# Attention rounds with whole-row maxima, strips of 256 queries, and the value products of two key tiles together at the end of a round

## The reference, cut to what matters

```python
B, S, D = X.shape                      # 1, 1024, 256
H, Dh = 16, 16
Xn = (X - mu) * rsqrt(var + 1e-5) * ln_w + ln_b
Q, K, V = split(Xn @ W_in, 3)          # each (16 heads, 1024, 16)
Q, K = _rope(Q), _rope(K)              # first half of the channels is rotated
scores = einsum('bhqd,bhkd->bhqk', Q, K) / sqrt(16)
probs = softmax(scores, axis=-1)
ctx = einsum('bhqk,bhkd->bhqd', probs, V)
out = ctx @ W_out + X
...                                    # the later stages are not changed
```

## Time and profile before

| what | value |
|---|---|
| time, median of 3 runs | 1087.62 us (1085.27 to 1093.72) |
| profiled execution, first to last instruction (its span) | 1084.3 us |
| median time less that span | 3.3 us |
| first query-side score (L519), first key-side score (L533) | 28.0 us, 48.3 us |
| first and last value product (L547) | 53.5 us, 231.7 us |
| busy over the span: PE, DVE, ACT, POOL | 95%, 73%, 62%, 47% |

### The profile page before, as it was taken

How to read it: one execution, slowest core, us unless ns; L and a number is a source line. 1 busy time by engine, 2 the same in 40 slices (tenths; PEclk the granted TensorE clock), 3 DMA queues, 4 the chain that set the end, 5 groups by cost and what they waited for, 6 DMA issues and landing times. The chain is left out here.

```text
span 1084.3 us, 18619 instructions
## 1 busy us (share of the span) xinstructions
PE 1028.1 (95%) x6437; PEld 812.5 (75%) x6437; DVE 787.5 (73%) x1789; ACT 673.7 (62%) x1235; POOL 507.1 (47%) x457
## 2 busy tenths in 40 slices
PE   7999999989999997799999999999889999999997
PEld 5433333347888986699988998899789778888997
DVE  5789999836766856898999999998567465333843
ACT  4478888756544447788778878787456344333454
POOL 3252331114058561767686777777506000536544
PEclk9989999999999998899999999999899999999999
DMA  4533434205224300351113121221011123655100
GB/s 91 91 64 56 76 54 68 70 13 164 78 70 136 49 2 23 113 181 64 55 64 113 59 65 54 93 73 39 2 36 28 44 57 88 159 159 163 67 20 21
DMA packets 80633, 79.28 MB, mean 73 GB/s; under 512 B 29320, under 2 KB 67676, under 8 KB 80540
## 3 DMA queue, kind: packets, MB, share of 16 engines
q1 hardware_dynamic: 80228, 77.66, 27.0%
q10 hardware_dynamic: 312, 0.43, 0.3%
HBM read 65.51 MB, written 1.28 MB: 62 GB/s over the span
## 5 line engine op out<-in xcount | busy, mean ns | idle before, releaser
L682 ACT ACTIVATE attn_probs<-attn_rows_k 128x512 f32<-128x512 f32 x256 | 134.4, 605 | 37.2 <-PE attn_rows_k L533 37.0
L770 DVE TENSOR_REDUCE attn_row_max<-s_sum 128x1 f32<-128x512 f32 x171 | 111.8, 682 | 15.9 <-PE s_sum L519 13.3
L533 PE MATMUL attn_rows_k<-attn_q_stack,attn_k_stack 50*128 50x512 f32 x256 | 96.9, 465 | 5.7 <-ACT attn_probs L682 5.6
L2865 DVE TENSOR_TENSOR late_mids<-late_mids,late_bank 128x512 f32<-128x512 f32 (+1 forms) x50 | 34.4, 687 | 78.8 <-PE late_bank L67 75.8
L65 PE MATMUL late_bank<-net_x_part_low,late_w_T 128*128 128x512 f32 (+1 forms) x192 | 77.9, 406 | 0.0
L66 PE MATMUL late_bank<-net_x_part_low,late_w_T 128*128 128x512 f32 (+1 forms) x192 | 76.1, 396 | 0.0
L67 PE MATMUL late_bank<-net_x_part_low,late_w_T 128*128 128x512 f32 (+1 forms) x192 | 76.0, 396 | 0.0
L519 PE MATMUL s_sum<-attn_k_stack,attn_q_stack 48*128 48x512 f32 x171 | 72.8, 470 | 1.9 <-DMA attn_q_stack<-s_part 1.4
L1530 POOL TENSOR_TENSOR gold_mids<-gold_mids,s_later 128x512 f32<-128x512 f32 x32 | 51.9, 1659 | 46.2 <-DMA s_later<-gold_weights 46.2
L2770 ACT ACTIVATE late_mids<-late_bank 128x512 f32<-128x512 f32 (+1 forms) x50 | 29.9, 597 | 69.6 <-PE late_bank L67 69.5
L2966 POOL TENSOR_TENSOR late_mids<-late_mids,late_raw_w_T_last 128x512 f32<-128x512 f32 x22 | 29.8, 1378 | 89.7 <-DMA late_raw_w_T_last<-top_weights 89.7
(11 more groups left out here) (459 smaller groups left out, 3491.9 us busy)
## 6 DMA issues: line engine op xcount, KB each, us to landing
lin_mix<-decay_sums SPq DMA_DIRECT2D x16, 512.0 KB, 3.8
lin_q_dec<-decay_sums SPq DMA_DIRECT2D x16, 512.0 KB, 5.3
s_later<-gold_weights SPq DMA_DIRECT2D x16, 256.0 KB, 3.6
attn_k_stack<-s_part SPq DMA_DIRECT2D x30, 128.0 KB, 3.5
s_raw_ring<-in_L_ffn_Wg SPq DMA_DIRECT2D x12, 256.0 KB, 2.8
s_raw_ring<-in_L_ffn_Wu SPq DMA_DIRECT2D x12, 256.0 KB, 3.1
...
```

What stands on the lines that cost most here:

```text
L533: pe.matmul(ps_k[n % 3][:, :], k_stack[rows, h % SLOTS, t * P:(t + 1) * P], q_stack[rows, h % SLOTS, :], start=True, stop=True).then_inc(s ...
L682: act.activation(probs[:, kk % PB, side * HALF:(side + 1) * HALF], ps_k[n % 3][:, :], ACT.Exp)\
L770: dve.tensor_reduce(row_max[:, tile, half:half + 1], ps_q[n % 3][:, :], axis=AX, op=ALU.max)\
```

## The change

PSUM is divided in another way. The bank `ps_turn` goes. The query-side scores get whole rows: a tile of 128 queries by all 1024 keys over two banks (`ps_tile`, three such tiles for the first 12 and two after that), written by two matmuls and reduced by one DVE instruction of 1024 elements in place of two of 512 and a combining step. The key-side scores keep three banks, which now form a ring (`ring`) that also takes the transposes: `turn_ctx` and `turn_max` each use the next bank of the ring, in order. The loop is written in rounds of two key tiles instead of units of one. The strips of `ps_ctx` are now four quarters of 256 queries (`QUARTER`), and even and odd key tiles are summed in the same place, so a key tile takes four matmuls of 256 moving columns, `add_ctx` on POOL goes, `turn_ctx` has two transposes once a head, and ACT copies 256 columns of sums instead of 512 and 136 turned elements instead of 272. The two calls of `weigh` of a round stand together at the round's end, behind all eight score matmuls. `turn_max` stands behind them, in a head's first round. The first two row swaps and the loading of the ones are issued by ACT's queue instead of SP's, and the pieces of the projection are 512 columns wide, one for a round.

The core of the diff:

```diff
+        ps_pair1, ps_pair2 = s.ps("rows_q1", [P, T]), s.ps("rows_k01", [P, T])
+        ps_tile = [golden.both_sums, ps_pair1, ps_pair2]
+        ps_q = [b[:, n * HALF:(n + 1) * HALF] for b in ps_tile[0:2] for n in range(2)]
+        ps_k = [ps_pair2[:, n * HALF:(n + 1) * HALF] for n in range(2)] + [s.ps("rows_k2", [P, HALF])[:, :]]
         ps_ctx = s.ps("ctx", [P, HALF])
-        ps_turn = s.ps("turn", [P, HALF])
-        turn_max_ps = ps_turn[0:MROWS * NT, 0:P]
-        piece_ps = ps_turn[:, 0:HALF // 2]
+        sums = ps_ctx[:, 0:QUARTER]
...
+        ROUNDS = NT // 2
+        Q_ROUNDS = ROUNDS * NH
+        K_LAG, W_LAG = 7, 8
+        MAX_LAG, COPY_LAG, TURN_LAG, NORM_LAG = ROUNDS, W_LAG + ROUNDS, W_LAG + ROUNDS + 1, W_LAG + ROUNDS + 2
+        ROUNDS_ALL = ROUNDS * (NH - 1) + TURN_LAG + 1
+        PIECES = 6
...
+        def tile_bank(n):
+            return n % 3 if n < 2 * PIECES else n % 2
+        tile_before = {n: max((m for m in range(n) if tile_bank(m) == tile_bank(n)), default=None) for n in range(2 * Q_ROUNDS)}
...
+        K_SIDES = ((0, 1), (1, 1), (0, 0), (1, 0))
+        ring = []
+        for q, _, k, _ in rounds():
+            if k is not None:
+                ring += [("exped", 4 * k + 1), ("exped", 4 * k + 2)]
+            if head_at(q, TURN_LAG) is not None:
+                ring.append(("ctx_taken", head_at(q, TURN_LAG) + 1))
+            if k is not None:
+                ring += [("exped", 4 * k + 3), ("exped", 4 * k + 4)]
+            if q < PIECES:
+                ring.append(("piece_copied", q + 1))
+            if head_at(q, MAX_LAG) is not None:
+                ring.append(("max_copied", head_at(q, MAX_LAG) + 1))
+        ring_first = ring.index(("exped", 1))
+        def ring_bank(job):
+            n = ring.index(job)
+            return ps_k[2 if n < ring_first else (n - ring_first) % 3]
+        def ring_before(job):
+            n = ring.index(job)
+            before = n - 1 if n <= ring_first + 2 else n - 3
+            if n in (ring_first, ring_first + 1):
+                return None
+            return ring[ring_first - 1] if n == ring_first + 2 else ring[before] if before >= 0 else None
...
+                def ring_free(job):
+                    before = ring_before(job)
+                    if before is not None:
+                        done = {"exped": exped, "ctx_taken": ctx_taken, "piece_copied": piece_copied, "max_copied": max_copied}
+                        pe.wait_ge(done[before[0]], before[1])
+                    return ring_bank(job)
...
+                def score_rows_q(q, side, half):
+                    h, r = divmod(q, ROUNDS)
+                    n = 2 * q + side
+                    if r == 0 and side == 0 and half == 0:
                         pe.wait_ge(stacked[h % SLOTS], all_stacked(h))
...
-                    n = 2 * g + side
-                    if n >= 3:
-                        pe.wait_ge(maxed, n - 2)
...
+                    if half == 0 and tile_before[n] is not None:
+                        pe.wait_ge(maxed, tile_before[n] + 1)
                     rows = slice(side * SIDE_ROWS, side * SIDE_ROWS + QROWS)
-                    pe.matmul(ps_q[n % 3][:, :], q_stack[rows, h % SLOTS, r * P:(r + 1) * P],
+                    pe.matmul(ps_tile[tile_bank(n)][:, half * HALF:(half + 1) * HALF],
+                              q_stack[rows, h % SLOTS, r * P:(r + 1) * P],
...
-                def score_rows_k(kk, side):
-                    h, t = divmod(kk, NT)
-                    if t == 0 and side == 1:
+                def score_rows_k(k, n):
+                    h, r = divmod(k, ROUNDS)
+                    odd, side = K_SIDES[n]
+                    if r == 0 and n == 0:
                         pe.wait_ge(max_stacked, 16 * 2 * (h + 1))
                         if h == 0:
                             pe.wait_ge(ones_stacked, 16 * 2)
-                    n = 2 * kk + 1 - side
-                    if n >= 3:
-                        pe.wait_ge(exped, n - 2)
+                            pe.wait_ge(maxed, 2 * PIECES)
+                    out = ring_free(("exped", 4 * k + n + 1))
                     rows = slice(side * SIDE_ROWS, side * SIDE_ROWS + QROWS + MROWS)
-                    pe.matmul(ps_k[n % 3][:, :], k_stack[rows, h % SLOTS, t * P:(t + 1) * P], q_stack[rows, h % SLOTS, :],
+                    t = 2 * r + odd
+                    pe.matmul(out, k_stack[rows, h % SLOTS, t * P:(t + 1) * P], q_stack[rows, h % SLOTS, :],
                               start=True, stop=True).then_inc(scored_k, 1)
-                def weigh(w):
-                    h, p = divmod(w, NT // 2)
-                    pe.wait_ge(exped, 4 * (w + 1))
-                    if p == 0 and h >= 1:
+                def weigh(w, odd):
+                    h, r = divmod(w, ROUNDS)
+                    t = 2 * r + odd
+                    pe.wait_ge(exped, 4 * w + 3 + odd)
+                    if t == 0 and h >= 1:
                         pe.wait_ge(ctx_copied, h)
-                    for odd in range(2):
-                        for b in range(2):
-                            j = 2 * b + odd
-                            i = pe.matmul(ps_ctx[j * VW:(j + 1) * VW, :], v[:, 2 * p + odd, h, :],
-                                          probs[:, (2 * w + odd) % PB, b * HALF:(b + 1) * HALF],
-                                          start=(p == 0), stop=(p == NT // 2 - 1))
+                    for j in range(4):
+                        i = pe.matmul(sums[j * VW:(j + 1) * VW, :], v[:, t, h, :],
+                                      probs[:, (2 * w + odd) % PB, j * QUARTER:(j + 1) * QUARTER],
+                                      start=(t == 0), stop=(t == NT - 1))
                     i.then_inc(summed, 1)
...
-                for n, u, g, kk, w in units():
-                    if u == U_MAX and 1 <= n <= NH:
-                        turn_max(n - 1)
-                    if g is not None:
-                        score_rows_q(g, 0)
-                    if kk is not None:
-                        score_rows_k(kk, 1)
-                    if u in U_CTX and 3 <= n:
-                        turn_ctx(n - 3, U_CTX.index(u))
-                    if kk is not None:
-                        score_rows_k(kk, 0)
-                    if g is not None:
-                        score_rows_q(g, 1)
-                    if n * NT + u in PIECE_AT:
-                        project_piece(*PIECE_AT[n * NT + u])
+                for n, q, k, w in rounds():
+                    if k is None and q is not None:
+                        for half in range(2):
+                            for side in range(2):
+                                score_rows_q(q, side, half)
+                    if k is not None:
+                        for p in range(2):
+                            if q is not None:
+                                score_rows_q(q, 0, p)
+                            score_rows_k(k, p)
+                    if head_at(n, TURN_LAG) is not None:
+                        turn_ctx(head_at(n, TURN_LAG))
+                    if k is not None:
+                        for p in range(2):
+                            if q is not None:
+                                score_rows_q(q, 1, p)
+                            score_rows_k(k, 2 + p)
                     if w is not None:
-                        weigh(w)
-                    if n * NT + u in EARLY_AT:
-                        what, j = EARLY_AT[n * NT + u]
+                        weigh(w, 0)
+                        weigh(w, 1)
+                    if n < PIECES:
+                        project_piece(n)
+                    if head_at(n, MAX_LAG) is not None:
+                        turn_max(head_at(n, MAX_LAG))
+                    for what, j in EARLY_AT.get(n, ()):
                         {"turn": turn_early, "rows": add_rows, "project": project_early}[what](j)
...
+                stack_ones()
+                for n, q, k, w in rounds():
+                    if head_at(n, COPY_LAG) is not None:
+                        copy_ctx(head_at(n, COPY_LAG))
+                    if k is not None:
+                        exp(k, 0)
+                        exp(k, 1)
+                    if head_at(n, TURN_LAG) is not None:
+                        take_ctx(head_at(n, TURN_LAG))
+                    if k is not None:
+                        exp(k, 2)
+                        exp(k, 3)
+                    if n < PIECES:
+                        copy_piece(n)
+                        if n < 2:
+                            act.wait_ge(piece_copied, n + 1)
+                            swap_rows(act, n)
+                    if n < ROUNDS:
+                        norm_x(2 * n)
+                        norm_x(2 * n + 1)
+                    if head_at(n, MAX_LAG) is not None:
+                        copy_max(head_at(n, MAX_LAG))
...
+                def row_maxima(q, side):
+                    h, r = divmod(q, ROUNDS)
+                    n = 2 * q + side
```

(6 more changed lines are left out.)

229 lines of the change are left out of this document (82 added, 147 removed).

## The result

Over 20 runs of each, the changed kernel takes 1093.88 us (1089.99 to 1097.97) and the kernel before 1088.53 (1085.27 to 1093.72): a ratio of 1.0046 with a 95% interval of 1.0032 to 1.0060, that is 3.5 to 6.5 us more. The profiled execution has a span of 1091.9 us, against 1084.3.

What follows compares the result with a forecast made beforehand. The prediction took a closed chain between PE and ACT, 2.70 us a round, as the bound. Its terms, 9.2 - 0.2 + 0.7 - 0.4 - 1.4 = +7.9 us on 1087.6, gave 1095.5 us, range 1087 to 1105.

Steps and rivals of the forecast that it cites:

- The chain of four links: Ordinary round: exponential to fourth key-side score 0.65 us, to value products 0.43, products 1.00, to next exponential 0.62; sum 2.70.
- The ring: One round of a head's four: the bank for `turn_ctx` delays the fourth key-side score 0.49 us; `turn_max` adds 0.20.
- The value products: End of each round: twice four strips of 256 columns need 16 loads, costing 0.02 us a round, at most 0.16.
- The first rounds: Rounds at the start of the key side that have no transpose yet: -0.2 us.
- The jobs: The next stage's jobs and both turns stand bare behind the value products: +0.7 us (0 to +2).
- the start: Before the key side: shorter rounds, against six DMAs on ACT delaying piece copies 1.4 to 2 us twice: -0.4 us.
- the end: Block's end: transposes ahead of the last product go elsewhere, a smaller copy, fewer transposes, no `add_ctx`: -1.4 us.
- Bare loads (the first): Value products: the second tile's eight loads are not hidden, 0.16 us in each of 64 rounds, giving 1104.4 us; chance 0.17.
- The ring's wait absorbed (the second): The long round: another engine sets the chain, so the bank's 0.49 us costs only in part, giving 1088.2 us; chance 0.10.
- That the half-clock stretch would go (the third): Start of the key side: a denser start removes the half-clock stretch, some 3 us, giving 1092.5 us; chance 0.08.
- DVE as the bound (the fourth): Every round: DVE bound it through the third query-side bank; whole rows save 0.3 us a round, giving 1076; chance 0.05.

Runs made afterwards that it cites:

- Half maxima: The changed kernel with row maxima taken over only the first 512 elements of each tile: 1091.5 us, 1.0021 times the kernel before.
- the split order: The changed kernel with the even key tile's value products between the second and third key-side scores: 1083.49 us, again 1085.2; with the transposes moved too, 1080.86.

## Why the prediction was right

**What bounds.** The chain of four links held to 0.01 us a link, with ACT ending the wait for the fourth key-side score. Half maxima change no steady round, so DVE was off the path there.

**The ring.** Forecast 0.49 for the bank and 0.20 for the maxima's transpose; measured 0.48 and 0.21. Taking the transposes out takes 0.5 us off a head, and moving them trades 0.48 for 0.37.

**The value products.** Here a size was a little off: the forecast paid 0.02 us a round for the second set of loads, and the interval from the first load to the next score is 1.00 us in both kernels. The term is zero. The head is 11.51 instead of 11.57. Thirteen heads, from value products to value products, take 149.87 us (66.26 to 216.13) where 142.61 passed before (67.28 to 209.89): 0.56 a head, 8.4 us for fifteen in place of 9.2.

**The first rounds.** From the first key-side score to the first value products pass 4.48 us (48.05 to 52.53) where 5.25 did (48.28 to 53.53): -0.77, of which the forecast had -0.2, for transposes that aren't there yet. The rest I had not seen. In the old trace PE waits several times for single maxima there, and in the new order half maxima still take 0.6 us off this stretch, so DVE counts in it; that whole tiles are what saves the time was not tried.

**The jobs, the start and the end.** +0.7 forecast, 4.4 - 3.8 = +0.6 measured. The start: -0.4 forecast, -0.2 measured (48.28 to 48.05), -0.5 if counted from the first query-side score. That this came out is luck: the DMAs on ACT cost 0.6 us in all, where the forecast had 1.4 to 2 in each of two rounds, so the shorter rounds ahead won about 1.1 us where the forecast needed 3 to 4. Two terms were too large by as much, and cancelled. The end: -1.4 forecast, 4.47 - 2.91 = -1.56 measured.

**The sum.** What the trace shows is 8.4 + 0.6 - 0.8 - 0.2 - 1.6 = +6.4 us, and the next stage starts 6.5 us later (242.14 against 235.6). The span grew by 7.6; the other 1.1 us lie in later stages, which the change doesn't touch. The medians differ by 5.35, so the forecast of +7.9 for the difference was too large, above the interval of 3.5 to 6.5 us. The forecast time came nearer than that, to 1.6 us, because it was counted from 1087.62, the median of three runs, and that of twenty is 1088.53: this too is luck. At an equal clock the difference is 7.4.

**The rivals.** Bare loads (the first) are refuted by 0.59 us of loads inside 1.00 us of products, the same 1.00 as with eight loads before. The ring's wait absorbed (the second) by the 3.4 us rounds and by the kernel without transposes. That the half-clock stretch would go (the third) by PEclk 0.64 and 0.72 at 48 to 64 us; its price of 3 us was also mis-added, as 2.5 rounds of 1.43 us are 3.6. DVE as the bound (the fourth) by the half maxima. The rule of the Trainium skill, TensorE: Matmul & The Clock Gate, Part 3, that loads run beside matmuls only when the row groups differ, does not describe these products: 16 loads on all 128 rows are hidden.

**Where my expectations failed.** I had looked for 0.2 us a head or more from moving the transposes in the split order, and it brought none. The likely reason, read from the intervals and not tried, is that with the products split PE's own work sets the half round, so what stands on PE counts wherever it stands. With half maxima I had looked for no change beyond 1 us, and overlooked DVE at the start. For the swaps I had looked for 1 to 1.5 us and found 0.6.
